# A two-layer transformer step on Trainium2: three groups of loads alternated between the SP queue and the GpSimd queue

## The reference

```python
# layer 1, attention
q = _apply_rotary(q, sin, cos, scale)
k = _apply_rotary(k, sin, cos, 1.0 / scale)
retention = einsum('bhtd,bhsd->bhts', q, k) * dk ** (-0.5) * decay_mask
out = einsum('bhts,bhsv->bhtv', retention, v)
...
# layer 1, feed-forward
def absmean(W):
    gamma = mean(abs(W)) + EPS
    Ws = W / gamma
    return sign(Ws) * minimum(round(abs(Ws)), 1.0)
h = einsum('btd,hd->bth', x, absmean(W_fc))        # W_fc is 4096 x 1024
h = layernorm(gelu(h), ln_w, ln_b)
y = einsum('bth,dh->btd', h, absmean(W_proj))      # W_proj is 1024 x 4096
...
x = x + attention(xn) + feed_forward(xn)
```

## Time and profile before

| | us |
|---|---|
| median of 3 runs | 9818.65 (9794.75 to 10436.36) |
| the profiled execution | 9816.05 |
| its span, slowest core (core 2) | 9814.5 |
| spans of the 8 cores | 9765.4 to 9814.5 |
| TensorE busy | 6579.6 (67%) |
| VectorE busy | 2607.0 (27%) |
| ScalarE busy | 1642.7 (17%) |
| GpSimd busy | 348.6 (4%) |
| layer-1 attention, from its first table load to the last output product | 6171 to 8148 |
| rounding of the two weights | 8149 to 8891 |
| feed-forward block and store | 8891 to 9814 |

### The profile page before, as it was taken

One profiled execution on the slowest core, in us unless ns is written; L12 is line 12 of the kernel. 1 busy time (PEld: TensorE's weight loads), 2 busy tenths in 40 slices (PEclk: granted clock), 3 DMA queues, 4 the chain that ended last, 5 costly groups with the idle time before them and its releaser, 6 DMA issues.

```text
span 9814.5 us, 82112 instructions; the slowest of 8 cores (9765.4 to 9814.5 us)
## 1 busy us (share of the span) xinstructions
PE 6579.6 (67%) x27956; PEld 2834.9 (29%) x27956; DVE 2607.0 (27%) x4154; ACT 1642.7 (17%) x2701; POOL 348.6 (4%) x510
## 2 busy tenths in 40 slices
PE   4545546477777899999999997455555551015777
PEld 2323323233333344444444442111111110001222
DVE  4233232300000100111110013555555554432111
ACT  1122121210111122111112211111111110001111
POOL 0000101000000000000000000000000000000000
PEclk5655656588888999999999998777777775557998
DMA  1311303199999534334334342111111104422222
GB/s 37 33 18 18 35 0 35 20 198 208 193 200 200 166 150 153 142 146 157 143 142 154 146 150 82 35 26 26 26 26 26 26 21 116 139 74 62 89 77 95
DMA packets 418873, 929.69 MB, mean 95 GB/s; under 512 B 169871, under 2 KB 301455, under 8 KB 340642
## 3 DMA queue, kind: packets, MB, share of 16 engines
q0 software_dynamic: 262080, 419.49, 20.8%
q1 hardware_dynamic: 156386, 504.95, 14.5%
HBM read 949.54 MB, written 159.38 MB: 113 GB/s over the span
## 4 chain that ended last, share of the span: by engine, by line
PE 54%; DVE 19%; DMA 15%; issue 6%; ACT 5%; DVEq 1%; SPq 0%; ACTq 0%; POOL 0%; POOLq 0%
PE psC L1057 8%; PE psE L1096 8%; PE psD L1057 8%; PE psF L1096 7%; DMA arena_bf<-w 4%; DMA arena_bf<-w2lay 3%; DMA arena_f<-wfcT 2%; DVE arena_f L828 2%; DMA arena_f<-wprojT 2%; DVE xres L1473 1%; DVE arena_f L851 1%; PE psD L1650 1%; PE psF L1725 1%; PE psC L1650 1%; PE psE L1435 1%
## 5 line engine op out<-in xcount | busy, mean ns | idle before, releaser
L1057 PE MATMUL psC<-xn,arena_bf 128*128 128x512 bf16 x4096 | 1022.8, 395 | 219.8 <-DMA arena_bf<-w 210.5
L1096 PE MATMUL psE<-arena_bf 128*128 128x512 bf16 x4096 | 957.9, 394 | 143.9 <-DMA arena_bf<-w2lay 111.2
L1057 PE MATMUL psD<-xn,arena_bf 128*128 128x512 bf16 x4096 | 985.5, 384 | 0.0
L1096 PE MATMUL psF<-arena_bf 128*128 128x512 bf16 x4096 | 904.9, 379 | 6.9 <-DMA arena_bf<-w2sc 3.9
L1109 DVE TENSOR_TENSOR arena_f<-psE,arena_f 128x512 f32<-128x512 f32 x128 | 88.5, 692 | 2961.7 <-PE psE L1096 2961.7
L1072 ACT ACTIVATE arena_bf<-psC,b1lay_s 128x512 bf16<-128x512 f32 x512 | 351.9, 687 | 2767.3 <-PE psC L1057 2767.3
L1057 PEld LDWEIGHTS psC<-xn,arena_bf 128*128 128x128 bf16 x4096 | 404.5, 100 | 749.8 <-issue 311.8
L1096 PEld LDWEIGHTS psE<-arena_bf 128*128 128x128 bf16 x4096 | 408.8, 101 | 681.9 <-issue 243.3
L1057 PEld LDWEIGHTS psD<-xn,arena_bf 128*128 128x128 bf16 x4096 | 407.4, 99 | 506.5 <-issue 41.3
L1096 PEld LDWEIGHTS psF<-arena_bf 128*128 128x128 bf16 x4096 | 399.3, 98 | 494.6 <-issue 17.0
L1072 ACT ACTIVATE arena_bf<-psD,b1lay_s 128x512 bf16<-128x512 f32 x512 | 351.9, 687 | 547.9 <-PE psD L1057 547.8
(11 more groups left out here) (324 smaller groups left out, 7302.8 us busy)
## 6 DMA issues: line engine op xcount, KB each, us to landing
arena_bf<-w1sc POOLq DMA_DIRECT2D x96, 1024.0 KB, 5.4
arena_bf<-w1sc SPq DMA_DIRECT2D x96, 1024.0 KB, 5.5
arena_bf<-w2sc SPq DMA_DIRECT2D x96, 1024.0 KB, 5.4
arena_bf<-w2sc POOLq DMA_DIRECT2D x96, 1024.0 KB, 5.3
arena_bf<-w POOLq DMA_DIRECT2D x64, 1024.0 KB, 14.4
w1sc<-arena_bf SPq DMA_DIRECT2D x64, 1024.0 KB, 8.2
arena_bf<-w2lay POOLq DMA_DIRECT2D x64, 1024.0 KB, 11.3
w2sc<-arena_bf SPq DMA_DIRECT2D x64, 1024.0 KB, 9.3
```

Of the source, the lines that this page charges most:

```text
L1057: p.op("pe", (lambda w1u, kc, fc, t0, psb: lambda e: e.matmul(psb[:, 0:512], w1u[:, kc * 512 + fc * 128: kc * 512 + (fc + 1) * 128], CH(K. ...
L1096: p.op("pe", (lambda w2u, fk, psb: lambda e: e.matmul(psb[:, 0:512], w2u[:, fk * 128:(fk + 1) * 128], h_all[:, fk * 512:(fk + 1) * 512], s ...
```

## The change

The choice of queue is changed for three groups of loads, and nothing else: buffers, sizes, waits for slots and the arithmetic stay.

- In `rotary_decay` the cosine and sine tables of odd g move from SP to POOL, and the positions of even g move from SP to POOL.
- In the first pass of `quant_weight` the chunks with odd index move to POOL.
- In the second pass too. The stores stay on SP.

Lines below the first edit stand 1 to 3 lines lower in the changed kernel (L1550 becomes L1553, L1590 becomes L1593).

```diff
@@ rotary_decay
+        qeng = "sp" if g % 2 == 0 else "gp"
-        ct = p.dma("sp", (lambda cs_s, csn, h, g: lambda e: e.dma_start(
+        ct = p.dma(qeng, (lambda cs_s, csn, h, g: lambda e: e.dma_start(
...
-        st_ = p.dma("sp", (lambda sn_s, snn, h, g: lambda e: e.dma_start(
+        st_ = p.dma(qeng, (lambda sn_s, snn, h, g: lambda e: e.dma_start(
...
-        pt = p.dma("sp", (lambda g: lambda e: e.dma_start(
+        pt = p.dma("gp" if g % 2 == 0 else "sp", (lambda g: lambda e: e.dma_start(
...
@@ quant_weight, first pass and, alike, second pass
-            dt = p.dma("sp", (lambda sl, r, c: lambda e: e.dma_start(
-                sl, K.ins[name][r * 128:(r + 1) * 128,
-                                c * chcols:(c + 1) * chcols]))(sl, r, c),
+            dt = p.dma("sp" if idx % 2 == 0 else "gp",
+                (lambda sl, r, c: lambda e: e.dma_start(
+                    sl, K.ins[name][r * 128:(r + 1) * 128,
+                                    c * chcols:(c + 1) * chcols]))(sl, r, c),
```

## The result

The changed kernel is faster by 1.1%: the ratio of its time to that of the kernel before is 0.9892, 95% interval 0.9857 to 0.9928. The predicted 9693 us against 9816 is a ratio of 0.987, inside that interval. The interval leaves out 1, and the whole of it lies inside the 2% that the chances called "within 2%". The profiled execution took 9676.42 us against 9816.05 before, 140 us less, where 123 were forecast.

A forecast was written before the change was run, and what follows sets the result against it. Neither VectorE nor DMA was taken to bound the second passes: each load waits on SP behind a store that waits for VectorE. Terms -147 + 10 + 14 = -123 took 9816 to 9693 us; range 9640 to 9785.

The forecast's parts named there:

- within 2%: Whole kernel: time changes by less than about 2%, 196 us, what a measurement can tell from no change; chance 96%.
- The second passes, -147 us: Rounding stage, second passes: odd chunks load ahead on POOL, 32 of 64 waits remain; -147 us, bounds -163 and -102.
- The sharing: Second passes: POOL's and SP's loads partly share the engines, costing 12.8 us in fc and 3.2 us in proj.
- The first passes, +10 us: Rounding stage, first passes: slower POOL loads cost 16 us, less the weight-unit wait; +10 us, bounds -29 and +37.
- I take 0.5 longer: First passes: a 512 KB load on POOL lands 0.5 us later than on SP, making each chunk 0.25 us longer.
- The 6 us that were to come back with the weight unit: proj's first pass: the feed-forward block's first weight unit goes out later on POOL, so a 6.0 us wait goes.
- Rival D: First passes: POOL's landing eats the gain from 13.5 us on; at 15 us it costs 163, time 9840; 3%.
- The attention, +14 us: Layer-1 attention: V's weights go out behind tables on POOL, costing 1.8 us in each of 8 heads; bounds 0, +67.
- the third starts 1.0 us late: Start of V in a head: late weights delay the third tile 1.0 us, taken as 1.8 with what lands beside.
- A: Both queues: they only share the engines, nothing is gained but the issue of 32 loads, 15 us; 9825 us; 4%.
- B: Second passes and attention: sharing in full and V's weights late, -46 us in all, 9770 us; 17%.
- C: Whole change: no cost anywhere, -163, half the first-pass waits gone (-14), V covered in full; 9639 us; 13%.

## Why the prediction was right in size and wrong in two of its terms

**The size, and luck in it.** 123 us were forecast and 140 measured, but not because every term was right. All terms were read on core 2, the slowest before, and core 2 itself fell by 149 us, from 9814.5 to 9665.1. The slowest core afterwards is core 4, which spent the longest of all, 6197 us, in the part ahead of the attention that nobody edited. In the means of the cores the rounding met its forecast, -138.5 against -137, because the second passes gave 7 us less than forecast and the first passes cost some 8 us less.

**The second passes, -147 us.** Right in mechanism and nearly in size. On core 2 they gave 333.3 - 181.7 - 3.5 = 148 us, in the mean of the cores 322.0 - 178.9 - 3.5 = 140 us. That the waits halve, and the gap of 0.1 us between two chunks, are as read from the trace. The sharing was taken as 0.8 us for each wait of fc and 0.2 of proj, 16 us in all: 333.3 - 166.6 + 16 = 182.7 us of waits, and 181.7 were measured on core 2. In the mean of the cores they waited less before (322 us), so halving gave less, and the sharing was a little dearer: 179 - 161 = 18 us. That it is sharing, and not the two stores in a row, the run with the POOL load held back has shown.

**The first passes, +10 us.** Right in both directions and wrong in both sizes. The step "I take 0.5 longer" for a landing on POOL was mis-sized: on core 2 the median landings are 5.5 us on POOL against 5.3 on SP in fc's pass and 4.3 against 4.5 in proj's, and an issue takes 0.53 us there, not the 0.88 of the weight loads. The nearest rows were loads with a cast or of twice the size, and neither was near enough. What alternating costs is 3 us a pass, 0.1 us a chunk and not 0.25. The 6 us that were to come back with the weight unit were 3. Together the first passes took 1.5 us more than before. Rival D, POOL's landing in the first passes, falls with it: the 13.8 us of the earlier trace rows belonged to that transfer and not to the queue.

**The attention, +14 us.** Wrong, and wrong in direction, in the step "with the weights at 7430.1 the two tiles, 1.87 us each, are done at 7433.9, so the third starts 1.0 us late". That step itself held: in the changed kernel V started at 7432.13 on core 2, 19.9 us after K's start and 0.3 us off the forecast, and the third tile began 23.2 us after K's start against 22.3. What failed is that a later third tile was counted as a later end, with the tiles behind it as long as before. V's tiles in the sixth head of the changed kernel, core 2:

```profile
7432.13 1.87 PE L1283 MATMUL psE<-arena_bf,xn 128*128 128x256 bf16 x8 [9.51 <-DMA arena_bf<-wqkv]
...
7437.21 1.48 PE L1283 MATMUL psF<-arena_bf,xn 128*128 128x256 bf16 x8
7438.52 1.04 PE L1283 MATMUL psE<-arena_bf,xn 128*128 128x256 bf16 x8
```

and of the kernel before, behind the pause in V of the earlier trace rows:

```profile
7436.22 1.76 PE L1282 MATMUL psE<-arena_bf,xn 128*128 128x256 bf16 x8
7437.82 1.04 PE L1282 MATMUL psF<-arena_bf,xn 128*128 128x256 bf16 x8
```

A tile is eight matmuls; those of 1.9 us ran at a granted clock of 0.50 (the lower level), those of 1.04 us at 1.00. K began at 7412.27 and 7410.53, so the first tile wholly at 2.4 GHz came 26.3 us after K's start in the changed kernel and 27.3 before. The fourteen tiles from the third on took 13.7 us and not 14.7, and V ended no later: K and V took 36.9 us against 37.1. The price of the start was right, and the clock paid it back. The gain on top of it, 7 us over the eight heads, comes mostly from heads in which V starts within 20 us of K. Of the 1.3 us that such a head gains, about 1.0 lies in K and V; the 0.3 behind them are not explained.

**The rivals.** A, that the queues only share the engines and nothing is gained, falls with the second passes. The Trainium skill's rule on it (DMA: Bandwidth & Descriptors, "Issuing engines are not separate DMA queues"), that DMAs issued from several engines run on the same DMA engines and save only the time to issue, agrees with the runs once the order is mended: with the loads ahead, one queue does what two do, 428 and 426 us. The second queue helped because it parted loads from the stores directly ahead of them; it did so even where it had stores of its own (482 us), as each load then stood behind the store of the chunk two earlier. B and C were sizes. The measured time, 9676, lies between the forecast and C's 9639, though C's conditions did not hold: the loads did share, and the waits of the first passes did not go (25.2 us in the mean against 24.4). What the prediction did not see at all is that SP alone could have had all of it.

## What to carry to other kernels

A queue that issues in order is a place in which a transfer waits for what stands ahead of it. Where a load stands behind a store that waits for computing, buffers for loading ahead are worth nothing; look for it wherever an engine waits for every single load and the DMA share is low, and put the loads ahead of the stores in the order of issue, before giving them another queue. Where a delay falls into a pause that was there already, work out the end of the phase and not only its start: the tiles behind the pause need not take as long as before.

## What was not expected of the hardware

- On POOL a load of 512 KB without a cast is issued in 0.53 us and lands in 4.3 to 5.5 us in the median of the first passes, much as on SP (0.33 us to issue, 4.5 to 5.3 us to landing). With a cast an issue took 0.88 us. Alternating 32 such loads between the queues cost 3 us in all.
- Two loads of 512 KB that go out 1.3 us apart cost the later one 1.2 us in fc, against runs in which the other went out 5.7 us behind it (6.2 and 5.0 us a wait).
- 256 KB stored and 512 KB loaded every 3.05 us, 257 GB/s at a DMA share of 0.83, leave VectorE without a wait behind the first chunk or two, on all 8 cores at once and from one queue alone.
- A pause of TensorE can cost less ahead of a run of matmuls than inside it: 19.77 + 15.65 = 35.4 us against 9.46 + 27.61 = 37.1 us for the same K and V phases. The lower figure had V whole at 2.4 GHz, the higher one had it at a granted clock of 0.75 in the mean. It is not always so: over the six later heads of that run K and V took 36.9 us, as before.
